# Six experts of a graph kernel on one core: eight of ten blocks routed to their chosen experts through rows sorted in DRAM, and a list schedule for the stage

## The reference, cut

```python
x = x + gnn(layernorm(x))                 # agg = segment_sum(H[src, etype], dst)
# mixture of six, D = H = 256, on f = layernorm(x)
rh = relu(f @ router_w1 + router_b1)
expert_logits = softmax(rh @ router_w2 + router_b2)
top_w, top_i = top_k(expert_logits, 2)
routing_weights = softmax(top_w)
h1 = relu(einsum('bsd,edh->bseh', f, expert_w1) + expert_b1)
h2 = relu(einsum('bseh,ehf->bsef', h1, expert_w2) + expert_b2)
expert_out = einsum('bsef,efo->bseo', h2, expert_w3) + expert_b3
x = x + sum(take(expert_out, top_i) * routing_weights)
```

## Time and profile before

| | |
|---|---|
| time, median of 3 runs | 1727.44 us (1724.54 to 1735.62) |
| span of the profiled execution | 1668.6 us, 23723 instructions |
| median over that span | 58.8 us |
| experts' stage in the span | first gather 195.4 us, attention's first gather 817.6 us |
| TensorE, products | 1495.7 us, 90% |
| TensorE, weight loads | 1005.9 us, 60% |
| VectorE / ScalarE / GpSimd | 62% / 37% / 47% |
| DMA | 270.07 MB, mean 162 GB/s |

### The profile page before, as it was taken

The page is one execution under the profiler, slowest core; times in us unless marked ns, Lnnn a source line. Parts: engine busy times, 40 slices in busy tenths (PEclk is TensorE's granted clock), DMA queues, the critical chain, the costliest instruction groups (busy, mean ns, idle before and its releaser), DMA issues. The chain is left out here.

```text
span 1668.6 us, 23723 instructions
## 1 busy us (share of the span) xinstructions
PE 1495.7 (90%) x6795; PEld 1005.9 (60%) x6795; DVE 1028.6 (62%) x2542; ACT 615.6 (37%) x1534; POOL 781.2 (47%) x738
## 2 busy tenths in 40 slices
PE   4999788999999999998356799999999999999996
PEld 2554314665666777777233467767766767767785
DVE  6543244345445555545388789898898888896432
ACT  3121002333234343443022355554555445555341
POOL 1100277646755777600378666574746556540000
PEclk9999857999999999999556699999999999999997
DMA  8448456546766566631487885665757565641100
GB/s 258 164 161 261 142 151 172 154 115 191 213 175 180 166 190 178 164 94 47 137 252 216 267 253 165 193 180 167 208 152 212 143 196 169 179 122 39 29 7 9
DMA packets 191573, 270.07 MB, mean 162 GB/s; under 512 B 28295, under 2 KB 156035, under 8 KB 188867
## 3 DMA queue, kind: packets, MB, share of 16 engines
q1 hardware_dynamic: 148419, 144.77, 27.7%
q0 software_dynamic: 43008, 123.61, 26.8%
HBM read 196.22 MB, written 72.06 MB: 161 GB/s over the span
## 5 line engine op out<-in xcount | busy, mean ns | idle before, releaser
L1890 POOL DMA_INDIRECT att_kv<-table_kv,g_srcI x314 | 368.5, 1174 | 246.4 <-issue 180.4
L1149 POOL DMA_INDIRECT ex_hg<-table_h,z_idx x314 | 316.7, 1008 | 150.2 <-issue 84.9
L2441 PE MATMUL att_psR<-g_mw,att_h 128*128 128x256 f32 x640 | 163.9, 403 | 1.0 <-ACT att_h L2259 1.0
L2414 PE MATMUL att_psR<-att_t,g_mw 128*128 128x256 f32 (+1 forms) x640 | 154.8, 387 | 0.1
L1466 PE MATMUL ex_psG<-ex_hg,ex_oh 128*42 128x256 f32 x628 | 134.6, 427 | 13.3 <-DMA ex_hg<-table_h,z_idx 7.2
L751 PE MATMUL tab_psH<-e_u,tab_xT 128*128 128x512 f32 x320 | 142.6, 598 | 4.3 <-DVE e_u L532 4.3
L2441 PEld LDWEIGHTS att_psR<-g_mw,att_h 128*128 128x128 f32 x640 | 124.7, 200 | 23.0 <-ACT att_h L2259 4.0
L1387 ACT ACTIVATE ex_h<-ex_psH,g_cols 128x256 f32<-128x256 f32 (+1 forms) x240 | 97.3, 464 | 93.8 <-PE ex_psH L1488 93.1
L2414 PEld LDWEIGHTS att_psR<-att_t,g_mw 128*128 128x128 f32 x640 | 121.2, 199 | 16.6 <-issue 2.6
L1882 POOL DMA_DIRECT2D table_o<-att_part x59 | 54.2, 919 | 161.9 <-DMA table_o<-att_part 90.5
L2301 PE MATMUL att_psG<-att_kv,att_oh 128*42 128x264 f32 x628 | 109.5, 431 | 13.7 <-DVE att_kv L1997 13.3
(11 more groups left out here) (308 smaller groups left out, 2465.1 us busy)
## 6 DMA issues: line engine op xcount, KB each, us to landing
table_h<-tab_hs SPq DMA_DIRECT2D x20, 1024.0 KB, 4.0
att_eft<-in_eft SPq DMA_DIRECT2D x158, 64.0 KB
ex_db<-table_dst SPq DMA_DIRECT2D x79, 126.0 KB
table_ohT<-ex_ohT SPq DMA_DIRECT2D x79, 126.0 KB
att_ohT<-table_ohT SPq DMA_DIRECT2D x79, 126.0 KB
table_oh<-ex_oh SPq DMA_DIRECT2D x79, 84.0 KB, 2.3
att_oh<-table_oh SPq DMA_DIRECT2D x79, 84.0 KB, 4.0
table_kv<-ex_qkv SPq DMA_DIRECT2D x10, 512.0 KB, 4.8
```

Of the source, the lines that this page charges most:

```text
L1149: nc.gpsimd.indirect_dma_start(hg[:, t % RING0, :], None, d.h[:, :], bass.IndirectOffsetOnAxis(ap=g.idx0[:, t:t + 1], axis=0)).then_inc(go ...
L1890: nc.gpsimd.indirect_dma_start(kv[:, t % (RINGC * TP), H:H + 2 * D], None, d.kv[:, :], bass.IndirectOffsetOnAxis(ap=g.srcI[:, t:t + 1], ax ...
L2414: ins = nc.tensor.matmul(out[:, c * CB:c * CB + used(b)], g.mw1[:, e, k, c * P:(c + 1) * P], t3[:, k, 0:used(b)], start=(k == 0), stop=(k ...
L2441: ins = nc.tensor.matmul(out[:, q * D:(q + 1) * D], h1[:, n % 3, k, q * P:(q + 1) * P], g.mw2[:, e, k, :], start=(k == 0), stop=(k == DK - 1))
```

## The change

Blocks 0 and 9 stay dense. Blocks 1 to 8 are in three parts (1 to 3, 4 to 6, 7 and 8). For each of their rows the place in a list of the rows of its two chosen experts is worked out (`choices`, `ranks`: a product with a triangle of ones, `positions`), and GpSimd scatters the normalized row to both places in DRAM (`scatter`, four indirect DMAs a block). When a part's last block has its positions, VectorE makes a table of which expert each slot of 128 sorted rows belongs to (`table`), for a fixed number of slots (17, 17, 13). SyncE loads a slot (`sL`); TensorE transposes it and runs the expert's three layers, with rows as the stationary side and the expert's weights, found by a register (`experts`), as the moving side; VectorE copies each layer's result from PSUM (`sA`, `sB`, `sC`), and it is transposed back for ScalarE's bias and relu (`tA`, `tB`). The result is stored (`sS`), GpSimd fetches two rows for each node (`fetch`, four indirect DMAs a block), and VectorE adds them by their weights (`combine`). The bias of layer C and the sums go straight into x (`mixed`), without `acc`. The tables' stage also writes zeros over all of the sorted rows (10,496 of 1 KB). PSUM banks are handed out by the plan, five in a pool. All orders, GpSimd's too, come from `plan0`, a list schedule over costs and dependencies (`pieces0`) that runs when the program is built; a join stands where its store has landed in the plan. The rest of `pieces0` lists waits of the same kind, `drained` waits for the bank's last holder.

```diff
+DENSE0, PARTS0 = (0, 9), ((1, 2, 3), (4, 5, 6), (7, 8))
+SPARSE0 = [b for part in PARTS0 for b in part]
+PART0 = {b: p for p, part in enumerate(PARTS0) for b in part}
+CAP0 = [sum(B0[b] for b in part) * P for part in PARTS0]
+SLOTS0 = [2 * cap // P + E0 - 1 for cap in CAP0]
+AT0 = [sum(SLOTS0[:p]) for p in range(len(PARTS0) + 1)]
+AREAS = [max([E0 * cap + (E0 - 1) * P for cap in CAP0[j::2]] + [P]) for j in range(2)]
+AREA0 = [p % 2 * AREAS[0] for p in range(len(PARTS0))]
+SXROWS = sum(AREAS)
...
+                    if tile >= 2:
+                        each = SXROWS // P // (NT - 2)
+                        n = each if tile < NT - 1 else SXROWS // P - (NT - 3) * each
+                        at = (tile - 2) * each * P
+                        sp.dma_start(d.sx[at:at + n * P, :].rearrange("(t p) c -> p t c", p=P),
+                                     zero[:, 0:D].unsqueeze(1).to_broadcast([P, n, D])).then_inc(cleared, 16)
...
+COST0 = {"gather": 4.1, "join": 0.95, "scatter": 4.2, "fetch": 4.2,
+         "group": 1.66, "turn": 0.62, "hidden": 1.05, "logits": 0.52, "rank": 0.35, "gateT": 0.38, "bias": 0.90,
+         "experts": 1.20, "sX": 0.31, "sA": 0.96, "tA": 0.31, "sB": 0.96, "tB": 0.31, "sC": 0.96, "A": 1.90, "B": 1.90, "C": 1.90, "turn2": 0.62, "q": 2.90}
...
+RANK0 = {"route": 3.5, "slots": 27.3, "pace": 0.8, "dense": 35.7, "post": 65.4, "fetch": 1.4}
+HOP, LANDS = 0.15, 2.4
...
+    for i in range(groups):
+        at = float(i)
+        add("POOL", "gather", i, 0, at, after("PE", "group", i - RING0 // TP))
+        add("DVE", "prepare", i, 0, at, after("PE", "group", i if i <= NSG // 2 else i - 1), after("SP", "keep", i - 2, 0, LANDS), after("DVE", "prepare", i - 1))
...
+        if sorts:
+            add("PE", "rank", b, 0, at, after("DVE", "choose", b))
+            add("DVE", "pos", b, 0, at, after("PE", "rank", b))
+            p = PART0[b] - 2
+            again = after("PE", "sX", AT0[p + 1] - 1, p) if p >= 0 and b == PARTS0[PART0[b]][0] else after("", "", -1)
+            add("POOL", "scatter", b, 0, at, after("DVE", "pos", b), after("DVE", "normed", b), again)
+            if b == PARTS0[PART0[b]][-1]:
+                add("DVE", "table", PART0[b], 0, at, after("DVE", "pos", b))
...
+    for b in DENSE0:
+        at = 8.0 * b + RANK0["dense"]
+        for e in range(E0):
+            slots_before = [p for p, part in enumerate(PARTS0) if part[-1] < b]
+            add("PE", "A", b, e, at + e, after("ACT", "turn", b), after("PE", "sC", AT0[slots_before[-1] + 1] - 1, slots_before[-1]) if slots_before else after("", "", -1))
+            add("ACT", "A", b, e, at + e, after("PE", "A", b, e), after("PE", "B", b, e - 2) if e >= 2 else after("", "", -1))
...
+        at = 8.0 * part[-1] + RANK0["slots"]
+        add("PE", "experts", p, 0, at, after("DVE", "table", p))
...
+            add("SP", "sL", n, p, at + RANK0["pace"] * j, prior("PE", "sX", XR), after("DVE", "table", p), *(after("POOL", "scatter", b, 0, LANDS) for b in part))
+            add("PE", "sX", n, p, at + RANK0["pace"] * j - 0.3, after("SP", "sL", n, p, LANDS), prior("PE", "sX", 1), after("PE", "experts", p),
+                *(after("PE", "C", b, E0 - 1) for b in DENSE0 if b < part[0]))
+            add("ACT", "sX", n, p, at + RANK0["pace"] * j, after("PE", "sX", n, p), prior("PE", "sA", 2))
+            add("PE", "sA", n, p, at + RANK0["pace"] * j, after("ACT", "sX", n, p), prior("PE", "sA", 1))
+            add("DVE", "sA", n, p, at + RANK0["pace"] * j - 20.0, after("PE", "sA", n, p), prior("PE", "tA", 2))
+            add("PE", "tA", n, p, at + RANK0["pace"] * j - 0.5, after("DVE", "sA", n, p))
...
+            add("POOL", "fetch", b, 0, at + RANK0["fetch"], *(after("SP", "sS", m, p, LANDS) for m in range(AT0[p], AT0[p + 1])),
+                after("DVE", "combine", SPARSE0[n - 2] if n >= 2 else -1), after("DVE", "table", p))
...
+    while any(open_.values()):
+        best = None
+        for engine, pieces in open_.items():
+            for piece in pieces:
+                start = max(free[engine], ready[piece])
+                if engine == "PE" and piece[1] in HELD0:
+                    start = max(start, min(banks))
+                if start < float("inf") and (best is None or (start, work[piece][1]) < best[0]):
+                    best = ((start, work[piece][1]), piece)
+        (start, _), piece = best
+        engine, what, b, e = piece
...
+        xsT, h1T, h2T = h1[:, 0, :, :].rearrange("p k (a c) -> p a k c", a=2), h1[:, 1, :, :].rearrange("p k (a c) -> p a k c", a=2), \
+            h2[:, 0, :, :].rearrange("p k (a c) -> p a k c", a=2)
+        ha = h2[:, 1, :, :]
...
-                        if i < JOINED_FROM:
-                            return
...
-                    for t in range(TE):
-                        if t >= RING0 and t % TP == 0:
-                            pool.wait_ge(s.summed, (t - RING0) // TP + 1)
-                        nc.gpsimd.indirect_dma_start(hg[:, t % RING0, :], None, d.h[:, :],
-                                                     bass.IndirectOffsetOnAxis(ap=g.idx0[:, t:t + 1], axis=0)).then_inc(got[t % RING0], 16)
-                        if t >= RING0 and t % TP == 0:
-                            join((t - RING0) // TP)
-                    for i in range((TE - 1 - RING0) // TP + 1, NG):
-                        join(i)
...
+                def scatter(b):
+                    pool.wait_ge(s.pos_ready, sparse(b) + 1)
+                    pool.wait_ge(s.xn_ready, b + 1)
+                    if PART0[b] >= 2 and b == PARTS0[PART0[b]][0]:
+                        for j in range(XR):
+                            pool.wait_ge(x_got[j], count(AT0[PART0[b] - 1], XR, j))
+                    for q in range(B0[b]):
+                        for j in range(2):
+                            nc.gpsimd.indirect_dma_start(d.sx[:, :], bass.IndirectOffsetOnAxis(ap=pos[:, T0[b] + q, j:j + 1], axis=0),
+                                                         xn[:, b % 2, q, :], None).then_inc(scattered[PART0[b]][b % 2], 16)
...
+                def fetch(b):
+                    pool.wait_ge(s.back_ready, PART0[b] + 1)
+                    for j in range(YR):
+                        pool.wait_ge(y_stored[j], count(AT0[PART0[b] + 1], YR, j))
+                    if sparse(b) >= 2:
+                        pool.wait_ge(s.combined, sparse(b) - 1)
+                    for q in range(B0[b]):
+                        for j in range(2):
+                            nc.gpsimd.indirect_dma_start(yf[:, sparse(b) % 2, q, j, :], None, d.sy[PART0[b]][:, :],
+                                                         bass.IndirectOffsetOnAxis(ap=ypos[:, T0[b] + q, j:j + 1], axis=0)).then_inc(fetched[sparse(b) % 2], 16)
...
+                def positions(b):
+
+                    n, p = sparse(b), PART0[b]
+                    i = PARTS0[p].index(b) * BT0
+                    u = Tally(s.pos_chain, n, 5, 2)
+                    ranks = psR[:, bank["rank", b, 0], :]
+                    dve.wait_ge(s.rank_made, n + 1)
+                    dve.wait_ge(s.places, 1)
+                    if b == PARTS0[p][-1]:
+                        nc.vector.tensor_scalar(nI[:, 0, :], ranks[:, BT0 * E0:BT0 * E0 + E0], float(P - 1), None, ALU.add)
+                    nc.vector.tensor_tensor(rk[:, :, :], ranks[:, 0:BT0 * E0].rearrange("p (t e) -> p t e", e=E0),
+                                            g.first0[:, p, :].unsqueeze(1).to_broadcast([P, BT0, E0]), ALU.add).then_inc(s.rank_taken, 1)
+                    dve.wait_ge(s.rank_taken, n + 1)
+                    for j in range(2):
+                        ins = nc.vector.tensor_tensor(kp[:, j, :, :], r.k[:, j, :, :], rk[:, :, :], ALU.mult)
+                    u.mark(ins)
+                    u.wait(dve)
+                    nc.vector.tensor_copy(kpart[:, :, i:i + BT0, :], r.k[:, :, :, :])
+                    u.mark(nc.vector.tensor_reduce(place[:, :, i:i + BT0], kp[:, :, :, :], AX.X, ALU.add))
+                    u.wait(dve)
+                    u.mark(nc.vector.tensor_copy(pos[:, T0[b]:T0[b + 1], :].rearrange("p t j -> p j t"), place[:, :, i:i + BT0]))
+                    nc.vector.tensor_copy(g.spare[0:1, 6:7], g.eps[0:1, 0:1]).then_inc(s.pos_ready, 1)
+                    assert u.base + u.n == u.per
+
...
+                def combine(b):
+                    n = sparse(b)
+                    dve.wait_ge(fetched[n % 2], 64 * (n // 2 + 1))
+                    dve.wait_ge(s.mixed_in, b + 1)
+                    for j in range(2):
+                        if j == 1:
+                            dve.wait_ge(s.half_combined, n + 1)
+                        for q in range(B0[b]):
+                            t = T0[b] + q
+                            ins = nc.vector.scalar_tensor_tensor(out=g.x[:, t, :], in0=yf[:, n % 2, q, j, :], scalar=keep[:, t, j:j + 1], in1=g.x[:, t, :],
+                                                                 op0=ALU.mult, op1=ALU.add)
```

(39 more changed lines are left out.)

691 lines of the change are left out of this document (522 added, 169 removed), and 5 rows, old and new, of the table BLOCK0.

## The result

The changed kernel takes 1836.82 us (median of 4, 1825.22 to 1845.52), the kernel before 1726.81 in the same series (1724.54 to 1735.62): a ratio of 1.061, interval 1.0550 to 1.0669. It is slower by 6%, where the forecast was 1736 and the range ended at 1778. Sign and mechanism are nearest to rival 2, whose far end was 1780.

What follows compares the result with a forecast made beforehand. It took TensorE as full and GpSimd as close to a bound, 78 us to spare. Last gather 712 plus tail 113.5 ended the stage at 825.5, 8 us later; span 1676.6 plus 58.8 gave 1735.4, say 1736 us; range 1706 to 1778.

Steps and rivals of the forecast that it cites:

- rival 2: Experts' stage: the list's waits on GpSimd, over 30 us in all, make it slower, 1755 to 1780; 0.35 with rival 3, the clock.
- Sum: 3 + 50 + 28 + 6 + 26.5 = 113.5 us: Tail behind the last gather: part 2's start, slots, block 9's experts, projections, ending; 113.5 us against 116.5 now.
- Thirteen slots: Tail: thirteen slots at 3.35 us are 44 us, taken as 50 with block 9's router and earlier projections between.
- So part 2 begins its slots 3 us behind the last gather: Tail: block 8's sums, router, scatters and slot load finish so that part 2's slots start 3 us behind the last gather.
- The last term: Tail's end: 26.5 us, as now, from block 9's normalization to the attention stage.
- The upper case: Tail: 130 us if projections of blocks 4 to 6, 17 us, are left over.
- The 81 us between are its slack: GpSimd up to the last gather: 81 us of waits, about 78 to spare, nearly all spent on its new work.
- Seven scatters and six fetches lie ahead of the last gather: GpSimd ahead of the last gather: 52 new DMAs at 1.30 us, 68 us.
- The 15 us for all waits: GpSimd's line: waits of scatters, fetches and joins with gathers queued behind, 15 us in all, bounds 0 and 60.
- Freeing TensorE can give back no more than 9 us: Experts' stage: TensorE is freed of 86 us, but GpSimd's remaining slack lets only 9 us come back.
- Rival 1: Experts' stage: TensorE was the bound and GpSimd finds room; 19 to 26 us earlier, say 1706 us; chance 0.20.
- an outside part of 58.8 us: Whole kernel: the median before exceeds the profiled span by 58.8 us, left as it is in the forecast.

Runs made afterwards that it cites:

- b1_extra_gathers: Kernel before with 53 extra indirect gathers on GpSimd, one to each group from the 26th, into a tile nobody reads; 1763.90 us, 1.0251.
- e3_plain_moves: Changed kernel with its 32 scatters and 32 fetches as plain transfers of the same size to and from fixed rows; 1805.65 us, 1.0442.
- e0_before: The kernel before, unchanged, run for a second profile; 1744.97 us, span 1743.5 us.
- e6: Changed kernel with every matmul of part 0's 17 slots done twice; 1839.28 us, 1.0664.
- e2: Changed kernel with each slot's expert a constant, so no register loads and no wait for the table; 1832.77 us, 1.0571.
- e10: Changed kernel with block 1 alone routed and nine blocks dense, planner's costs unchanged; 1829.84 us, 1.0539.
- after: The changed kernel itself, eight blocks routed, as profiled and timed; 1836.82 us, 1.0610 against the kernel before.
- e14: e10 with dense experts and block tails due earlier in the planner's priorities; 1842.76 us, 1.0755.
- e15: Changed kernel, eight blocks routed, with slots, dense experts and block tails due earlier in the planner's priorities; 1850.84 us, 1.0765.
- e13: Changed kernel with all planner costs that the rows contradict set to the rows; 1835.74 us, 1.0652.
- e4: Changed kernel with GpSimd's planner costs set to the rows: gather group 5.1 for 4.1, join 1.25, scatter and fetch 5.2; 1841.09 us, 1.0688.
- e5: As e4, but with 6.2 for a group of gathers; 1899.30 us, 1.1001.
- e12: Changed kernel with the eight routed blocks in four parts of two, at e4's prices; 1875.49 us, 1.0822.
- e11: As e10, but planner costs 6.9 for a group of gathers, 1.25 for a join, 5.2 for a scatter or fetch; 1788.52 us, 1.0335.
- e9: Changed kernel with only blocks 1 to 3 routed and seven dense, at e4's prices; 1823.29 us, 1.0589.
- e7: Changed kernel with twelve small unread matmuls added behind each of groups 0 to 28 and 34 to 41; 1849.05 us, 1.0747.
- e8: Changed kernel with the twelve fetches of part 0 spread behind gathers 69, 72 and 75; 1841.47 us, 1.0719.

## Why the prediction was wrong

**The tail: the step that failed first.** "Sum: 3 + 50 + 28 + 6 + 26.5 = 113.5 us": measured 190.5. By its terms: up to block 9's experts 119.8 us for 3 + 50; block 9's experts 28.9 for 28; from there to the attention 41.8 for 6 + 26.5. The middle term was right, the first was out by 67 us. "Thirteen slots" were 20, 7 x 3.35 = 23 us; six tiles of projections at 2.8 us stand among them, 17 us; TensorE is idle 14 us of the stretch; some 12 us are left for the clock of 0.90 and block 9's router. For all but the slots the 50 held 6 us. The 3 failed too, "So part 2 begins its slots 3 us behind the last gather": its first load is issued 27 us behind it. Block 8's last gather of group 72 was issued 43 us ahead of the last of all (735.64), near the 36 of the prediction, but from there to the load of the block's sums it took 38 us, for the "some 12 us" of landing, sum, halves, store, join and load, and 25 more to the positions, for 16. TensorE filled that time with part 1's slots, so the delay and the left-over slots are one loss, not two. The last term has eight projections, where I took four with half of them hidden. I followed only the rows of block 8 through the tail, at the pace of an empty machine, as if the order had finished everything before them by then. It had not: it puts gathers first whenever they are ready, and what the gathers leave goes behind them. The upper case that I gave, 130 us with some projections left over, has the right mechanism and a fifth of its size.

**"The 81 us between are its slack."** As a sum of waits it was right, and as a budget it was wrong: I set 68 us of new DMAs against 78 us of slack and charged 11. The 68 was wrong as well: "Seven scatters and six fetches lie ahead of the last gather" were seven and three, 40 transfers and 51 us. b1_extra_gathers measured 0.76 us for each 1.33 us of such work, 40 us for 53; e3_plain_moves got 31 us back for 45 us taken off that line. In the changed kernel itself the last gather is 31 us later than in e0_before, where my step had +11: the point from which rival 2 decides, more than 30 us of held line, is passed. The 15 us for all waits of scatters, joins and fetches were too few: the scatters alone waited 27.5 us for positions ahead of the last gather (31.6 less the 4.1 of the last one), and the first fetch 8.5.

**"Freeing TensorE can give back no more than 9 us."** Not contradicted: e6 puts 35 us more of products on TensorE and the time moves by no more than the intervals. Rival 1 falls with the result itself.

**The level.** The sum stood on an execution that was 46 us early at the last gather and that I lifted to the median by an outside part of 58.8 us. The last gather of 712 was therefore out by 67 us against the 778.6 measured, of which 46 are this. It didn't decide the direction of the forecast, since the outside part held the same 46, but it hid that TensorE is not full in every execution (45.6 of 50 between 450 and 500).

**What held.** The tables' stage, +2 forecast and +2.4 measured; 1.30 us for a scatter or fetch (1.33 and 1.27 measured); no cost of loads from registers that can be told from noise (e2, 4 us against bounds of 0 to 28); TensorE clearly under 95% busy from 300 to 700, at 71%. Two of the signs did not come. TensorE is not "idle for gathers": from 200 to 770 it waits 6.5 us for gathered rows, 24.8 for VectorE's one-hot matrices and 54.7 ahead of the groups for nothing that the profile names. GpSimd's waits for its sums did not fall under 20 us (36.0, and 26.8 of "remote"). So GpSimd was not the bound that the sum was built on. The 141 new copies from PSUM on VectorE do not show in GpSimd's gathers: 984 ns on average here, 993 in e0_before, 1,008 in the earlier trace rows. The Trainium skill, page "SBUF — State Buffer", section "SBUF: two separate sides", names a float32 copy from SBUF to SBUF as one that stops GpSimd's descriptors, and no copy from PSUM; the trace doesn't contradict it. The 5 us that I had added for longer gathers were not needed.

**What the cause is, and how far it is shown.** Shown: at the change's own prices the routing is not what costs most, since one routed block costs as much as eight (e10 against after; e14 against e15 at earlier, not quite equal, ranks); neither more work on TensorE (e6), nor the register loads (e2), nor the planner's prices alone (e13) make the loss; plain transfers in place of the 64 indirect DMAs take some 31 us off it (e3); and with the same blocks routed every order that shortens the tail by over 10 us lengthens the stretch before it (e4, e5, e12 and e15 against after, e11 and e14 against e10). Not shown: that this holds at other prices. With GpSimd's group at 6.9 one routed block takes 1789 us (e11), with 6.2 eight take 1899 (e5), and three take 18 us less than eight at e4's prices (e9, e4): there the routed work costs much, and routing and order do not come apart. The reading that joins these is that fixed orders on five engines, made from one plan, turn each late step into a wait of all that is queued behind it, at four groups of lead. That was seen in single places (e5 at 475, after at 655 and 680), not proved for the whole. Open: which waits hold each group in the stretches from 24 to 60, where after and e0_before are equal in sum but not group for group; what of e10's loss belongs to the zeros (10.7 MB), the pool of five PSUM banks, the sums that go straight into x, the ring sizes and the places of the joins, which stay in it; and what the late signals of the last section cost. The kernel that would tell, the hand-written order of before with one block routed, wasn't tried.

## What to carry to other kernels

An engine's waits are not a budget for new work when the ring between it and its partner is short: price each hidden operation at half its duration or more (0.76 us of 1.33 in b1_extra_gathers, 0.5 to 0.7 of it by the interval; 31 us back for 45 in e3_plain_moves), unless a run shows less. Before an operation is exchanged to find its price, look at what its stand-in takes. When a change replaces a hand-written order by a planned one, take the plan's own end apart first: count each block's work that it leaves behind the last step of the bound stream; and split the change into "the new order with the old work" and "the new work in the old order", since here one routed block of eight, with all else of the change left in, cost as much as all of it. Take two profiles of the kernel before, where its span and its median lie further apart than its runs.

## What the runs showed of the hardware

**One kernel, two executions.** The profiles of the kernel before have spans of 1668.6 and 1743.5 us, 4.5% apart, and part from the 4th group on; seven timed executions on the chip of the second lie within 1.3% of each other.

**Signals from TensorE seen late.** In after, some groups' sums are released long after the last of their products has ended in the records, and for three engines at the same instant. Group 32, whose last product ends at 425.4, on ScalarE, VectorE and GpSimd:

```profile
424.77 0.63 PE L1933 MATMUL ex_psG<-ex_hg,ex_oh 128*42 128x256 f32 x2
...
431.89 0.37 ACT L1845 COPY ex_odd<-ex_psG 42x256 f32<-42x256 f32 x1 [6.92 <-remote]
...
431.89 0.33 DVE L1421 TENSOR_TENSOR ex_oh<-g_iotag,g_dstgrp 128x168 f32<-128x168 f32 x1 [7.57 <-remote]
...
432.13 0.94 POOL L1404 DMA_INDIRECT ex_hg<-table_h,z_idx  x1 [1.15 <-remote]
```

It is 6.5 us here and 12.6 at group 48 (product ends at 544.8, ScalarE starts at 557.36); some 24 groups, 95 us in sum, 80 of it while ScalarE stood idle. The same groups (32, 48, 54) are late in e2, e7 and e8. But the changed kernel is not alone in it. b1_extra_gathers, the kernel before but for its extra gathers, has 17 such groups with ScalarE idle, 63 us, and the first of them, as this one, come long before the first extra gather:

```profile
232.77 0.37 ACT L1408 COPY ex_odd<-ex_psG 42x256 f32<-42x256 f32 x1 [15.10 <-remote]
```

e0_before has seven, 32 us, up to 9.4 at group 3, and the execution of the earlier trace rows, the same program, has none: they are part of how the two executions differ. The number of them does not order the runs (e11 has three, 7 us, and its last gather comes at 804.3), so what they cost the changed kernel isn't shown. The ends of matmuls are modelled in these records, so it may be that TensorE itself was held there; the cause is open.

**Products that cost little.** 35 us more of matmuls on an engine that was busy 67 to 79% of the time (500 to 650) raised its granted clock from 0.81 to 0.93 (490 to 700) and moved the time by no more than the intervals (e6).

**Plain and indirect transfers on GpSimd.** 128 rows of 1 KB took it 1,026 ns to scatter and 965 ns to fetch, each with a pause of 0.30 us (after), and 574 and 552 ns as plain transfers of the same size (e3).
